# Placing tokens in expert tiles: the codes multiplied in on GpSimd, a quarter of the low one-hot columns made by ScalarE, signed codes and one sum

## What is computed

```python
def _L0_ffn_ref(x, router_w, w1, b1, w2, b2):
    E, C, F, K = (8, 192, 768, 2)
    flat = x.reshape(-1, Cc)
    probs = jax.nn.softmax((flat @ router_w.T).astype(jnp.float32), axis=-1)
    top_w, top_i = jax.lax.top_k(probs, K)
    top_w = (top_w / top_w.sum(-1, keepdims=True)).astype(x.dtype)
    out = jnp.zeros_like(flat)
    for e in range(E):
        w_e = jnp.sum(top_w * (top_i == e), axis=-1)[:, None]
        h = jax.nn.gelu(flat @ w1[e] + b1[e], approximate=False)
        out = out + w_e * (h @ w2[e] + b2[e])
    return out.reshape(B, T, Cc)
```

## Time and profile before

| what | value |
|---|---|
| median of 3 runs (lowest, highest) | 415.99 us (414.44, 416.58) |
| the profiled execution's own time | 412.6 us |
| its span | 410.5 us |
| mean granted TensorE clock, share of full speed | 0.979 |
| TensorE matmuls busy | 371.7 us, 91% |
| VectorE busy | 255.7 us, 62% |
| ScalarE busy | 212.4 us, 52% |
| GpSimd busy | 171.2 us, 42% |

### The profile page before, as it was taken

One profiled execution on the slowest core, in us unless ns is written; L12 is line 12 of the kernel. 1 busy time (PEld: TensorE's weight loads), 2 busy tenths in 40 slices (PEclk: granted clock), 3 DMA queues, 4 the chain that ended last, 5 costly groups with the idle time before them and its releaser, 6 DMA issues.

```text
span 410.5 us, 14839 instructions
## 1 busy us (share of the span) xinstructions
PE 371.7 (91%) x5722; PEld 328.0 (80%) x5722; DVE 255.7 (62%) x662; ACT 212.4 (52%) x431; POOL 171.2 (42%) x214
## 2 busy tenths in 40 slices
PE   4989999989999999997998889999999999999910
PEld 4989989979889899874453589999999999999800
DVE  4687468887877778785299255555455554455426
ACT  5668577778778786853210154444444444444400
POOL 8117322346455452317300545555555555553310
PEclk9999999999999999999999999999999999999965
DMA  8973004433334323361151203131322312222058
GB/s 261 350 222 140 17 21 128 133 97 92 102 116 118 86 81 95 107 186 34 51 136 45 52 28 96 55 88 53 88 57 82 85 55 88 59 54 47 30 208 331
DMA packets 29673, 42.82 MB, mean 104 GB/s; under 512 B 12384, under 2 KB 19408, under 8 KB 29608
## 3 DMA queue, kind: packets, MB, share of 16 engines
q1 hardware_dynamic: 25480, 33.37, 26.7%
q0 software_dynamic: 4128, 8.50, 7.6%
HBM read 30.23 MB, written 9.67 MB: 97 GB/s over the span
## 4 chain that ended last, share of the span: by engine, by line
PE 40%; DVE 6%; issue 6%; POOL 3%; DMA 3%; ACT 1%; SPq 0%; POOLq 0%; DVEq 0%
PE PSA L1240 19%; PE PSA L1255 15%; PE PSA L1124 2%; DMA W2h<-yrows 2%; POOL XF L473 2%; PE PSA L1259 2%; PE PSA L1207 2%; DVE PTR L920 1%; DVE H L987 1%; POOL REG L480 1%; DVE VB L918 1%; DMA yrows<-KBR 1%; DVE VB L914 1%; POOL REG L479 1%; SPq L440 0%
## 5 line engine op out<-in xcount | busy, mean ns | idle before, releaser
L1240 PE MATMUL PSA<-YT,W1h 128*128 128x128 f16 x774 | 78.0, 219 | 1.9 <-DVE YT L949 1.9
L1240 PE MATMUL PSA<-YT,W1l 128*128 128x128 f16 (+1 forms) x516 | 75.3, 220 | 0.0
L1255 PE MATMUL PSA<-W2h,PTR 128*128 x516 | 71.0, 246 | 0.3 <-DVE PTR L679 0.3
L510 POOL DMA_INDIRECT yrows<-KBR x43 | 43.0, 999 | 63.7 <-DVE KBR L964 63.7
L1240 PEld LDWEIGHTS PSA<-YT,W1h 128*128 x774 | 63.7, 98 | 6.0 <-DVE YT L949 2.2
L665 ACT ACTIVATE PTR<-PSA 128x768 f32<-128x768 f32 x43 | 34.8, 810 | 63.2 <-PE PSA L1240 63.2
L1255 PE MATMUL PSA<-W2l,PTR 128*128 x258 | 63.6, 246 | 0.0
L505 POOL DMA_INDIRECT REG<-xrows,KBR x43 | 42.4, 985 | 42.8 <-DVE KBR L941 26.6
L670 ACT ACTIVATE PTR<-PTR 128x768 f16<-128x768 f32 x43 | 36.3, 844 | 44.4 <-PE PSA L1259 44.3
L679 DVE SCALAR_TENSOR_TENSOR PTR<-PTR 128x768 f16<-128x768 f32 x43 | 41.2, 959 | 25.5 <-ACT PTR L670 25.5
L964 DVE TENSOR_SCALAR KBR<-PSA,KBR 128x192 f32<-128x192 f32 x43 | 18.0, 418 | 53.1 <-PE PSA L1259 53.1
(11 more groups left out here) (164 smaller groups left out, 793.8 us busy)
## 6 DMA issues: line engine op xcount, KB each, us to landing
WSTG<-w SPq DMA_DIRECT2D x16, 384.0 KB, 3.4
WSTG<-w SPq DMA_DIRECT2D x16, 336.0 KB, 3.2
REG<-xt SPq DMA_DIRECT2D x12, 324.0 KB, 5.1
W1l<-xt SPq DMA_DIRECT2D x10, 324.0 KB, 6.6
VB<-VP SPq DMA_DIRECT2D x99, 19.1 KB
H<-hrows SPq DMA_DIRECT2D x6, 288.0 KB, 2.8
xrows<-REG SPq DMA_DIRECT2D x1, 1600.5 KB
hrows<-H SPq DMA_DIRECT2D x1, 1296.0 KB
```

What stands on the lines that cost most here:

```text
L510: gp.indirect_dma_start(out=yrows, out_offset=bass.IndirectOffsetOnAxis(ap=TARGET[:, s:s + 1], axis=0), in_=YO[s % 2], in_offset=None).the ...
L1240: ins = nc.tensor.matmul(bank(2 * u + f // (FC // 2), 128, FC // 2 * ST_)[:, w:w + ST_], weights[a, c], YT[0:rows, at:at + ST_], start=k = ...
L1255: nc.tensor.matmul(bank(4 + u, ST_, C), GP[a][:, at:at + ST_], weights[b], start=(f, a, b) == (0, 0, 0), stop=False)
```

## The change

- The codes are multiplied into AT_HIGH by GpSimd, a quarter at a time. VectorE makes the high one-hots in two halves, each with its own signal, and no products.
- VectorE makes the low one-hots of three quarters. ScalarE makes the fourth: 11 activations Abs(LOW - iota), one for each column with LOW as bias, then one activation Relu(1 - that), which is 1 where the two are equal and 0 elsewhere.
- LOW is worked out from BITS, in parallel with HIGH.
- Codes are signed: the tokens of the first 11 tiles have codes -1188 to -1, the others 1 to 1188, so one sum in bank 5 over both choices tells the token, and 0 an empty slot. A second sum over the first choice alone (bank 4) tells ISFIRST.
- xrows has one more row, number 1188 (BLANK), of zeros, to which empty slots point. SOURCE is the sum plus 1188. The rows on either side of it are stored by two transfers each, and the blank row by one of its own.
- The unread matmuls before the last quarter are 2 instead of 6; GpSimd sets one more small constant (UNITY). The first gather waits for the stores (5 transfers) and for SOURCE.

```diff
 SPARE = NS * ST_
-CODED = 2048 // TT
-CODES = 2 * TOPK
+HALF = NT // 2
+BLANK = HALF * TT
 
...
         START = after(E)
-        LATE, FOUND = after(TOPK * NS), after(TOPK * NS)
-        ANY, ISFIRST, UNUSED, TWICE, GATE = [after(NS) for _ in range(5)]
+        ISFIRST, UPPER, UNUSED, TWICE, GATE = [after(NS) for _ in range(5)]
         SOURCE, TARGET = [after(NS).bitcast(U32) for _ in range(2)]
         JUNK2 = after(1)[0:1]
+        UNITY = after(1)[0:TT]
 
...
         HSTEP = NS + 1
+        APART = VP[:, 0:TOPK * NT * ST_ // 4]
         AT_LOW = PTR[0:TT, 0:TOPK * NT * ST_ // 2].bitcast(F16)
...
                 sp.dma_start(dst, src).then_inc(later_in, 16)
+            sp.dma_start(xrows[BLANK:BLANK + 1, :], blank).then_inc(rows_stored, 16)
             sp.wait_ge(w_lo, 2 * PIECES)
...
             sp.wait_ge(route, GATES)
-            for a, b in ((0, 96), (96, TT)):
-                sp.dma_start(xrows.rearrange("(t p) c -> p t c", p=TT)[a:b], RB[a:b].rearrange("p (t c) -> p t c", c=ROW)).then_inc(rows_stored, 16)
+            for n in range(2):
+                first = n * (BLANK + 1)
+                part = xrows[first:first + BLANK, :].rearrange("(t p) c -> p t c", p=TT)
+                for a, b in ((0, 96), (96, TT)):
+                    sp.dma_start(part[a:b], RB[a:b].rearrange("p (t c) -> p t c", c=ROW)[:, n * HALF:(n + 1) * HALF]).then_inc(rows_stored, 16)
             sp.wait_ge(h_stored, 16 * 2)
...
             nc.gpsimd.memset(CUM[1], 0.0).then_inc(ones_set, 1)
+            gp.wait_ge(ones_set, 3)
+            nc.gpsimd.memset(UNITY, 1.0).then_inc(ones_set, 1)
             gp.wait_ge(op_mm, NT)
-            gp.wait_ge(ones_set, 3)
+            gp.wait_ge(ones_set, 4)
             nc.gpsimd.memset(YT[CB:CX, :].rearrange("p (u c) -> p u c", u=2)[:, :, 3 * ST_:], S_X).then_inc(ones_set, 1)
...
 
-            gp.wait_ge(rows_stored, 16 * 2)
-            gp.wait_ge(table, 5)
+            for n, (a, b) in enumerate(PARTS):
+                gp.wait_ge(high_placed, n // 2 + 1)
+                if n == 0:
+                    gp.wait_ge(ones_set, 5)
+                nc.gpsimd.tensor_tensor(at_high(a, b), at_high(a, b), CODE[:, a:b].unsqueeze(2).to_broadcast([TT, b - a, NS]),
+                                        ALU.mult).then_inc(coded, 1)
+
+            gp.wait_ge(rows_stored, 16 * 5)
+            gp.wait_ge(table, 1)
             for s in range(FETCHED):
                 gather_rows(s)
-            gp.wait_ge(table, 10)
+            gp.wait_ge(table, 8)
             for s in range(NS):
...
 
+            act.wait_ge(ones_set, 4)
+            act.wait_ge(count, COUNTED)
+            a, b = PARTS[-1]
+            for n in range(a, b):
+                nc.scalar.activation(APART[:, (n - a) * ST_:(n - a + 1) * ST_], IOTA, ACT.Abs, bias=LOW[:, n:n + 1], scale=-1.0).then_inc(apart, 1)
+            act.wait_ge(apart, b - a)
+            nc.scalar.activation(at_low(a, b), APART.rearrange("p (n c) -> p n c", c=ST_), ACT.Relu, bias=UNITY, scale=-1.0).then_inc(apart, 1)
 
...
             nc.vector.tensor_copy(HIGH, BITS).then_inc(count, 1)
-            dve.wait_ge(count, 16)
-            nc.vector.scalar_tensor_tensor(LOW, HIGH, -float(ST_), SLOTF, ALU.mult, ALU.add).then_inc(count, 1)
+            nc.vector.scalar_tensor_tensor(LOW, BITS, -float(ST_), SLOTF, ALU.mult, ALU.add).then_inc(count, 1)
             dve.wait_ge(count, COUNTED)
-            nc.vector.tensor_tensor(at_high(0, TOPK * NT), IOTA[:, 0:NS].unsqueeze(1).to_broadcast([TT, TOPK * NT, NS]),
-                                    HIGH.unsqueeze(2).to_broadcast([TT, TOPK * NT, NS]), ALU.is_equal).then_inc(high_placed, 1)
-            dve.wait_ge(high_placed, 1)
-            for a, b in PARTS:
-                nc.vector.tensor_tensor(at_high(a, b), at_high(a, b), CODE[:, a:b].unsqueeze(2).to_broadcast([TT, b - a, NS]),
-                                        ALU.mult).then_inc(coded, 1)
+            for n in (0, 2):
+                a, b = PARTS[n][0], PARTS[n + 1][1]
+                nc.vector.tensor_tensor(at_high(a, b), IOTA[:, 0:NS].unsqueeze(1).to_broadcast([TT, b - a, NS]),
+                                        HIGH[:, a:b].unsqueeze(2).to_broadcast([TT, b - a, NS]), ALU.is_equal).then_inc(high_placed, 1)
+            for a, b in PARTS[:-1]:
                 nc.vector.tensor_tensor(at_low(a, b), IOTA.unsqueeze(1).to_broadcast([TT, b - a, ST_]),
                                         LOW[:, a:b].unsqueeze(2).to_broadcast([TT, b - a, ST_]), ALU.is_equal).then_inc(low_placed, 1)
 
             dve.wait_ge(table_mm, 1)
-            sums = bank(5, ST_, CODES * NS).rearrange("p (k h s) -> p k h s", k=TOPK, h=2)
-            late, found = [ap.rearrange("p (k s) -> p k s", k=TOPK) for ap in (LATE, FOUND)]
-            nc.vector.tensor_scalar(late, sums[:, :, 1, :], 0.0, float(TT * CODED), ALU.is_gt, ALU.mult).then_inc(table, 1)
-            nc.vector.tensor_reduce(found, sums.rearrange("p k h s -> p k s h"), AX.X, ALU.add).then_inc(table, 1)
+            found, first = bank(5, ST_, NS), bank(4, ST_, NS)
+            nc.vector.tensor_scalar(SOURCE, found, float(BLANK), None, ALU.add).then_inc(table, 1)
+            nc.vector.tensor_scalar(ISFIRST, first, 0.0, None, ALU.not_equal).then_inc(table, 1)
+            nc.vector.scalar_tensor_tensor(UNUSED, found, 0.0, SPAREROW, ALU.is_equal, ALU.mult).then_inc(table, 1)
+            nc.vector.tensor_scalar(UPPER, found, 0.0, -2.0, ALU.is_gt, ALU.mult).then_inc(table, 1)
             dve.wait_ge(table, 2)
-            nc.vector.tensor_tensor(FOUND, FOUND, LATE, ALU.add).then_inc(table, 1)
-            dve.wait_ge(table, 3)
-            nc.vector.tensor_tensor(ANY, FOUND[:, 0:NS], FOUND[:, NS:2 * NS], ALU.add).then_inc(table, 1)
+            nc.vector.scalar_tensor_tensor(TWICE, found, 2.0, ISFIRST, ALU.mult, ALU.subtract).then_inc(table, 1)
             dve.wait_ge(table, 4)
-            nc.vector.tensor_scalar(SOURCE, ANY, -1.0, 0.0, ALU.add, ALU.max).then_inc(table, 1)
-            nc.vector.tensor_scalar(ISFIRST, FOUND[:, 0:NS], 0.0, None, ALU.is_gt).then_inc(table, 1)
-            nc.vector.scalar_tensor_tensor(UNUSED, ANY, 0.0, SPAREROW, ALU.is_equal, ALU.mult).then_inc(table, 1)
+            nc.vector.tensor_tensor(UNUSED, UNUSED, UPPER, ALU.add).then_inc(table, 1)
             dve.wait_ge(table, 6)
-            nc.vector.scalar_tensor_tensor(TWICE, ANY, 2.0, ISFIRST, ALU.mult, ALU.subtract).then_inc(table, 1)
-            dve.wait_ge(table, 8)
             nc.vector.tensor_tensor(TWICE, TWICE, UNUSED, ALU.add).then_inc(table, 1)
-            dve.wait_ge(table, 9)
-            nc.vector.tensor_scalar(TARGET, TWICE, -1.0, None, ALU.add).then_inc(table, 1)
+            dve.wait_ge(table, 7)
+            nc.vector.tensor_scalar(TARGET, TWICE, 2.0 * BLANK + 1, None, ALU.add).then_inc(table, 1)
 
...
             unread(28)
-            codes_of = [(k, t // CODED) for k in range(TOPK) for t in range(NT)]
-            for n, (k, late) in enumerate(codes_of):
+            def placed(n, to, start, stop):
                 rows = TT if n % NT < NT - 1 else LAST
-                at = (2 * k + late) * NS
-                if n in PART_OF:
-                    unread(6)
-                    pe.wait_ge(low_placed, PART_OF[n] + 1)
-                    pe.wait_ge(coded, PART_OF[n] + 1)
-                ins = nc.tensor.matmul(bank(5, ST_, CODES * NS)[:, at:at + NS], AT_LOW[0:rows, n * ST_:(n + 1) * ST_],
-                                       AT_HIGH[0:rows, n * HSTEP:n * HSTEP + NS], start=(k, late) not in codes_of[:n],
-                                       stop=(k, late) not in codes_of[n + 1:])
+                return nc.tensor.matmul(bank(to, ST_, NS), AT_LOW[0:rows, n * ST_:(n + 1) * ST_],
+                                        AT_HIGH[0:rows, n * HSTEP:n * HSTEP + NS], start=start, stop=stop)
+
+            for p, (a, b) in enumerate(PARTS):
+                unread(6 if p < 3 else 2)
+                if p < 3:
+                    pe.wait_ge(low_placed, p + 1)
+                else:
+                    pe.wait_ge(apart, b - a + 1)
+                pe.wait_ge(coded, p + 1)
+                for n in range(a, b):
+                    ins = placed(n, 5, n == 0, n == TOPK * NT - 1)
+                if b <= NT:
+                    for n in range(a, b):
+                        placed(n, 4, n == 0, n == NT - 1)
             ins.then_inc(table_mm, 1)
...
             pe.wait_ge(bias_in, 16 * 3)
-            pe.wait_ge(ones_set, 4)
+            pe.wait_ge(ones_set, 5)
             expert = {}
...
         "iota": np.tile(np.arange(128), (TT, 1)).astype(np.float16),
-        "codes": np.tile(TT * (np.arange(NT) % CODED), TOPK)[None, :].repeat(TT, 0).astype(np.float32) + tok[:, None].astype(np.float32) + 1,
-        "spare": (np.arange(NS)[None, :] * ST_ + np.arange(ST_)[:, None] + TOPK * NT * TT + 1).astype(np.float32),
```

(7 more changed lines are left out.)

5 lines of the change are left out of this document (2 added, 3 removed).

## The result

The changed kernel took 412.70 us (median of 6 runs, 412.42 to 414.29) against 415.74 for the kernel before beside it (6 runs, 414.44 to 416.58): ratio 0.9924, 95% interval 0.9898 to 0.9951, or 3.0 us less. Forecast were 0.84 us less and 415.1, with 412.8 as the lower end: the time lies 0.1 under the range, and the change is beyond the 0.5% within which I had called it the same.

The account below looks back on a forecast made before the run. Bound by waits through VectorE alone while the token table is made, then TensorE. -0.64 (sums) - 0.20 (second gather) = -0.84: profiled 412.6 becomes 411.8, plus 3.4 carried over to the median, 415.1; range 412.8 to 417.4.

Parts of the forecast that it names:

- The turns: Table stage: GpSimd products and VectorE low comparisons alternate on shared ports, 2.36 us a round; chance 0.48, including gains to 2.1.
- No collision: Rival, table stage: GpSimd's products hardly delay VectorE's comparisons; gain 2.59 + 0.20, 413.2 us; chance 0.19.
- VectorE keeps the ports: Rival, table stage: GpSimd's first product waits for VectorE's last low comparison; +1.1 us, 417.1; chance 0.13.
- dear product: Rival, table stage: each GpSimd product takes 2.48 us; sums +4.9 - 0.2, 420.7 us; chance 0.07.
- Whole turns: Rival, table stage: GpSimd and VectorE each hold the ports for full instructions, without overlap; +0.4 us, 416.4; chance 0.10.
- Gain on the way to the sums: Table stage: the last table matmul ends at 224.74 instead of 225.38, 0.64 us gained.
- Gain 0.20: Behind the table: the earlier gather removes TensorE's 0.20 us wait for the second gather's rows; nothing else gained there.
- same within 0.5%: Whole kernel: the change of 0.2% stays within 0.5%, or 2.1 us, counted as no change; chance 0.68.
- Carrying over 3.4 us: Whole kernel: the median shown, 415.99, is 3.4 above the profiled 412.6; added to 411.8 it gives 415.1.
- ScalarE at nothing: Table stage: ScalarE's low quarter, 3.9 us of absolute values and 1.7 wide step, done by 219.6, costs nothing.
- Twice 0.58 for 22 matmuls: TensorE, table stage: each of the first two quarters issues 22 table matmuls instead of 11, taking 0.58 us each.
- SyncE's four stores: Row stores: four instead of two plus a blank row land by 220, before gathers at about 225; cost nothing.

Follow-up runs that it names:

- codes_only: The kernel before with only signed codes, blank row, single sums and short table: 412.17 us, ratio 0.9983 to the kernel before.
- late_gather: The changed kernel with its first gather waiting for all 8 table steps instead of the first: 415.42 us, ratio 0.9987 to the kernel before.
- no_gp: The changed kernel with products back on VectorE and one high comparison for all columns: 410.82 us, ratio 0.9954 to the kernel before.
- act_only: The kernel before with only ScalarE making the last low quarter and 2 unread matmuls before it: 414.89 us, ratio 0.9968.
- ts: no_gp with VectorE's comparisons made column by column, scalars from SBUF, code multiplied in by the same instruction: 419.02 us, ratio 1.0089 to the kernel before.
- b_held: The kernel before with two more 768-column copies on ScalarE before the first GELU: 416.83 us, ratio 1.0069 to the kernel before.
- codes_held: codes_only with two more 768-column copies on ScalarE before the first GELU: 414.84 us, ratio 1.0025 to the kernel before.

## Why the prediction was right and wrong

*The turns* were right, and they were the heart of it. Forecast from the first high comparison to the sums: 224.74 - 214.01 = 10.73; measured 10.65 to the end of the last table matmul (225.49 - 214.84), and 10.69 to the read. The round was put at 2.36 and is 2.32. The first product ran freely for 1.05 by the forecast's reading: it would have begun 0.21 before the second high comparison's end at 217.04, and it ended at 217.88. "No collision", "VectorE keeps the ports" and "dear product" are out by that. One sign came out only nearly: the last quarter began at 224.96, behind two unread matmuls, when the last product (done at 224.82) had just ended, and the chain of waits runs through TensorE from 221.72 on. Whole turns, the rule of the Trainium skill ("SBUF — State Buffer", section "SBUF: two separate sides"), would make a round 1.09 + 1.62 = 2.71. The trace agrees that one engine holds the other up for most of an instruction, and not that it does for all of it: about 0.4 us a round overlap at the handovers.

*Gain on the way to the sums*: forecast 0.64, of which 0.13 before the first comparison and 0.51 behind it; measured 0.59 behind it, and the 0.13 as well: from the cast of HIGH to the first comparison it is 0.33 (214.51 to 214.84) where it was 0.46.

*Second gather, "Gain 0.20"*: this step failed. It counted the wait that the row showed, and measured was 0.77 (7.48 to 6.71). Missed was what is queued behind the wait: the sequencer's address work, from 231.7 to the expert matmul at 232.90 in before, and done by 231.8 in after. codes_only (6.68) and late_gather (7.35) show the price from both sides.

*The sum* by the profiles is 0.13 + 0.59 + 0.77 = 1.49 where it was forecast 0.84, and the repeats gave 1.3, 1.5 and 1.6: closed to 0.2. In these three comparisons the forecast's "same within 0.5%" holds as well.

*Carrying over 3.4 us* from the profile to the median was the second failure, of another kind. It took the 415.99 of three runs for the kernel's time; the kernel's time moves between 413.0 and 416.2 from series to series. A range of 2.3 us to either side couldn't hold a gain of 1.5 and a move of the reference of that size. Of the 2.4 us between 415.1 and 412.70, 0.65 are the gain that the sum had missed, 0.25 the median of before in that comparison (415.74, not 415.99), and 1.5 are the part whose cause stays open. So the 0.20 alone would have left the time inside the range.

*ScalarE at nothing* was right: 11 absolute values in 3.32 us (3.9 allowed), the wide step 1.47, done at 219.72 and wanted at 224.96. No table load stands among them or between them and the first GELU, as the Trainium skill has it ("ScalarE: Activation LUTs", section "Table sets: the hidden batching unit"). *Twice 0.58 for 22 matmuls* was wrong for the second quarter, 1.02; in after it cost at most about 0.1 (the last quarter began 0.14 behind the last product), in no_gp it set the end. *SyncE's four stores* cost nothing: by window, the transfers of after were

```profile
217.00:219.00 2.00, 1.71 (x8) 0.58 (x6) 2.00 (x2) 1.97 (x6) 2.00 (x2) 1.00 0.63 183
219.00:221.00 2.00, 1.59 (x27) 1.06 (x28) 2.00 (x2) 0.72 (x1) 2.00 (x2) 1.00 0.03 10
```

still at 0.63 of the engines to 219 and over by 221, more than 5 us before the gather.

## What to carry to other kernels

Before moving work to GpSimd beside VectorE instructions with two SBUF inputs, set what it takes from VectorE against its own time less the handovers: here 0.56 us off VectorE for 1.09 on GpSimd was a loss. The same trade with ScalarE was a gain: a 1.53 us comparison went, and VectorE's rounds in act_only stayed at 2.10 us. Price a wait by what its engine's sequencer still has to do behind it, not by the idle time in its row. And before a difference of 1% is believed, run both kernels again on another occasion: here the median of one unchanged kernel moved by 0.8%.

## What the runs showed of the hardware that I had not expected

- A wait of 0.20 us on TensorE's side cost 0.77, through address work behind it that takes the sequencer 1.1 us (231.7 to 232.8 in before).
- Twenty-two table matmuls take 0.73 us in the first quarter and 1.02 in the second, with the same count and shapes (0.72 and 1.02 in after). Why wasn't tried.
- A VectorE comparison with scalars from SBUF costs, from one start to the next, 0.16 us for 128 columns with one scalar, and 0.20 for 43 columns with a second operation and a second scalar (ts).
- Holding ScalarE's first GELU back by two copies lowered TensorE's granted clock to 0.50 for about 3 us (b_held), some 1.9 us of time by codes_held, in 28 of 35 executions by their mean clock.
